# Adding the four ranks of expert outputs: quartered loads and one tiled product for a pair of row tiles

## The reference, cut to what matters

```python
out = jnp.zeros_like(xt)
for e in range(E):
    a = _swiglu(xt @ expert_up_w[e].T)
    out = out + cw[:, e:e + 1] * (a @ expert_down_w[e].T)
out = out + _swiglu(xt @ shared_up_w.T) @ shared_down_w.T
...
x = x + gb * ffn          # gb: one row of 256 for each of the two batches
```

## Time and profile before

| what | value |
|---|---|
| median of 3 runs | 631.35 us (630.82 to 632.19) |
| span of the profiled execution | 628.4 us |
| time outside that span, if the execution took the median | 2.95 us |
| TensorE busy | 576.8 us (92%) |
| VectorE busy | 477.5 us (76%) |
| ScalarE busy | 373.5 us (59%) |
| GpSimd busy | 341.5 us (54%) |
| mean granted TensorE clock | 0.986 |

### The profile page before, as it was taken

How to read it: one execution, slowest core, us unless ns; L and a number is a source line. 1 busy time by engine, 2 the same in 40 slices (tenths; PEclk the granted TensorE clock), 3 DMA queues, 4 the chain that set the end, 5 groups by cost and what they waited for, 6 DMA issues and landing times. The chain is left out here.

```text
span 628.4 us, 13726 instructions
## 1 busy us (share of the span) xinstructions
PE 576.8 (92%) x3945; PEld 390.7 (62%) x3945; DVE 477.5 (76%) x1406; ACT 373.5 (59%) x877; POOL 341.5 (54%) x646
## 2 busy tenths in 40 slices
PE   4997899999999999998987798898979999999987
PEld 4885543334343434443342387687869999999964
DVE  4968998888898778686948569799756776667767
ACT  4775576666676656555867564454546666666630
POOL 5114563646567554944648877781345555555550
PEclk9989999999999999997999989999999999999999
DMA  8389669864547480751115143774986444444983
GB/s 288 82 208 247 179 147 221 206 174 109 141 100 219 117 220 26 174 215 55 69 52 187 54 170 121 252 217 140 339 341 198 139 131 130 137 139 137 355 311 125
DMA packets 66083, 107.96 MB, mean 172 GB/s; under 512 B 13513, under 2 KB 52185, under 8 KB 63834
## 3 DMA queue, kind: packets, MB, share of 16 engines
q1 hardware_dynamic: 59146, 87.93, 48.5%
q0 software_dynamic: 6864, 19.15, 7.9%
HBM read 60.90 MB, written 43.88 MB: 167 GB/s over the span
## 5 line engine op out<-in xcount | busy, mean ns | idle before, releaser
L1458 ACT ACTIVATE Pr<-bank 128x512 f32<-128x512 f32 (+3 forms) x384 | 165.7, 494 | 97.9 <-PE bank L2261 94.1
L1574 DVE TENSOR_REDUCE mxA<-bank 128x1 f32<-128x128 f32 (+3 forms) x256 | 112.3, 482 | 20.9 <-PE bank L2148 20.6
L2261 PE MATMUL bank<-Qs,Ks 99*128 99x512 bf16 (+3 forms) x384 | 118.0, 331 | 6.0 <-ACT Pr L1458 4.2
L2148 PE MATMUL bank<-Ks,Qs 96*128 96x512 bf16 (+3 forms) x384 | 120.2, 330 | 1.2 <-DVE mxB L1574 0.6
L1280 POOL DMA_INDIRECT expert_rows<-Y,YIX x79 | 77.3, 978 | 78.5 <-ACT Y L1521 75.4
L1574 DVE TENSOR_REDUCE mxB<-bank 128x1 f32<-128x512 f32 x128 | 81.6, 681 | 13.8 <-PE bank L2148 13.8
L2247 PE MATMUL bank<-Pr,Vst 128*32 128x512 f32 (+3 forms) x768 | 83.0, 505 | 3.5 <-POOL Pr L1259 3.5
L1257 POOL TENSOR_TENSOR tick<-ident 128x1 f32<-128x1 f32 x128 | 25.5, 199 | 106.5 <-ACT Pr L1458 105.6
L2506 PE MATMUL bank<-W,xh 128*128 x316 | 78.0, 328 | 1.1 <-issue 1.1
L1209 POOL DMA_INDIRECT chosen_rows<-Hx,pos x64 | 67.6, 1056 | 19.2 <-issue 19.2
L2261 PEld LDWEIGHTS bank<-Qs,Ks 99*128 99x128 bf16 x384 | 35.9, 98 | 58.4 <-ACT Pr L1458 39.3
(11 more groups left out here) (256 smaller groups left out, 1278.3 us busy)
## 6 DMA issues: line engine op xcount, KB each, us to landing
G<-chosen_rows SPq DMA_DIRECT2D x79, 134.0 KB, 2.2
Z<-expert_rows SPq DMA_DIRECT2D x8, 1024.0 KB, 8.3
W<-expert_words SPq DMA_DIRECT2D x7, 1088.0 KB, 9.5
qk_parts<-AP SPq DMA_DIRECT2D x32, 192.0 KB, 3.1
Wraw<-in_wexp SPq DMA_DIRECT2D x9, 608.0 KB, 5.7
SA<-in_wexp SPq DMA_DIRECT2D x7, 608.0 KB, 4.3
Vst<-Vall SPq DMA_DIRECT2D x8, 512.0 KB, 5.3
expert_words<-SH SPq DMA_DIRECT2D x7, 480.0 KB, 3.6
```

The costliest lines, as they stand in the source:

```text
L1458: nc.scalar.activation(Pr[(2 * s + j // 2) % 4][:, j % 2, 0:w], ebank[p % RING][:, 0:w], ACT.Exp, scale=SCALE).then_inc(exp_done, EXP)
L1574: nc.vector.tensor_reduce(dst, mbank[u % RING][:, 0:w], AX.X, ALU.max).then_inc(m_red, 1)
L2148: nc.tensor.matmul(mbank[u % RING][:, 0:w], Qs[slot][0:NPR, i // TPC, j, (i % TPC) * P:(i % TPC + 1) * P], Ks[slot][0:NPR, j, k0:k0 + w], ...
L2261: nc.tensor.matmul(ebank[p % RING][:, 0:CH - q0], Ks[slot][0:NAUG, j, kt * P:(kt + 1) * P], Qs[slot][0:NAUG, qc, j, q0:CH], start=True, st ...
```

## The change: what it does

- Loads: each rank is loaded by quarters of 32 partitions. Quarter c of rank r (the tokens of 32 output partitions) goes to slot c of `Z`, at the 32 partitions (r + c) mod 4. So slot c holds on its 128 partitions the same 32 x 16 tokens of all four ranks. Ranks 0 to 2 take 4 DMAs of 512 KB each, in place of 2 of 1 MB; the last rank takes 4 parts of 4 row tiles, each of 4 quarters: 16 DMAs of 128 KB. In all 28 DMAs in place of 8, of the same bytes.
- TensorE: `fold` is a 128x32 matrix with ones where partition and column agree modulo 32. For each of the 8 pairs there are four products, one for each slot, of 128x32 by 128x512, each into its own band of 32 partitions of one bank. One product adds the four ranks of a quarter. VectorE makes `fold` once, at block 8 of the loop, from the identity.
- VectorE multiplies each of the 8 banks by the gate (the last in two halves), and adds pairs 0, 1, 3, 5, 7 to `X`; it adds no ranks any more. GpSimd adds pairs 2, 4 and 6 to `X`, behind its last scatter.
- SP issues the outputs in the order of the pairs, behind waits for VectorE's or GpSimd's add.

```diff
-PE_PAIRS, DVE_PAIRS = (1, 2, 4, 6, 7), (0, 3, 5)
-END_ORDER = (0, 3, 1, 2, 5, 4, 6, 7)
-Z_PARTS = 2
+PAIRS = NT // 2
+LAST_PAIR = PAIRS - 1
+POOL_ADDS = (2, 4, 6)
+DVE_ADDS = tuple(k for k in range(PAIRS) if k not in POOL_ADDS)
+QUARTERS, QP = 4, P // 4
+LAST_PARTS = 4
+Z_PARTS = [1] * (SUMS - 1) + [LAST_PARTS]
...
-            n = NT // Z_PARTS
-            queue.dma_start(Z[:, r, i * n:(i + 1) * n, :],
-                            zd[r * T:(r + 1) * T, :].rearrange("(p n) h -> p n h", n=NT)[:, i * n:(i + 1) * n, :]
-                            ).then_inc(z_in[r * Z_PARTS + i], 16)
+            n = NT // Z_PARTS[r]
+            rows = zd[r * T:(r + 1) * T, :].rearrange("(p n) h -> p n h", n=NT)
+            for c in range(QUARTERS):
+                at = (r + c) % QUARTERS * QP
+                queue.dma_start(Z[at:at + QP, c, i * n:(i + 1) * n, :],
+                                rows[c * QP:(c + 1) * QP, i * n:(i + 1) * n, :]
+                                ).then_inc(z_in[sum(Z_PARTS[:r]) + i], 16)
...
-            for k in END_ORDER:
-                if k in DVE_PAIRS:
-                    sp.wait_ge(z_step, ADD_STEPS * (DVE_PAIRS.index(k) + 1))
+            for k in range(PAIRS):
                 tiles = [(2 * k, 2)] if k != LAST_PAIR else [(2 * k, 1), (2 * k + 1, 1)]
                 for t, n in tiles:
-                    if k in PE_PAIRS:
-                        sp.wait_ge(fin_done, PE_PAIRS.index(k) + 1 + t % 2)
+                    if k in POOL_ADDS:
+                        sp.wait_ge(pool_added, POOL_ADDS.index(k) + 1)
+                    else:
+                        sp.wait_ge(fin_done, DVE_ADDS.index(k) + 1 + t % 2)
...
+            def add_gated(k):
+                pool.wait_ge(s_gated, 2 * NC + k + 1)
+                t = slice(2 * k, 2 * k + 2)
+                nc.gpsimd.tensor_tensor(X[:, t, :], X[:, t, :], Z[:, 0, t, :], ALU.add).then_inc(pool_added, 1)
...
+            def make_fold():
+                dve.wait_ge(mp_step, NIT * 9)
+                nc.vector.tensor_reduce(fold, ident[:, :].rearrange("p (c t) -> p t c", c=QUARTERS), AX.X,
+                                        ALU.add).then_inc(fold_made, 1)
...
-            for k in END_ORDER:
-                if k in DVE_PAIRS:
-                    add_pair(DVE_PAIRS.index(k), k)
-                if k in PE_PAIRS and k != LAST_PAIR:
-                    finish(PE_PAIRS.index(k), 0, 2)
+            for k in range(LAST_PAIR):
+                gate_sums(k, 0, 2)
+                if k in DVE_ADDS:
+                    add_gated(k, 0, 2)
             for first in range(2):
-                finish(PE_PAIRS.index(LAST_PAIR), first, 1)
+                gate_sums(LAST_PAIR, first, 1)
+                add_gated(LAST_PAIR, first, 1)
...
-                for r in range(SUMS):
-                    ins = nc.tensor.matmul(allb[i + u][:, 0:n * H], ident[:, :],
-                                           Z[:, r, t:t + n, :].rearrange("p t h -> p (t h)"), start=(r == 0), stop=(r == SUMS - 1))
+                if k == LAST_PAIR:
+                    pe.wait_ge(y_read, NB)
+                for c in range(QUARTERS):
+                    ins = nc.tensor.matmul(allb[k][c * QP:(c + 1) * QP, :], fold,
+                                           Z[:, c, 2 * k:2 * k + 2, :].rearrange("p t h -> p (t h)"), start=True, stop=True,
+                                           skip_group_check=True)
                 ins.then_inc(z_ps, 1)
```

More of the change, by code:

```diff
@@ L331 @@
 COUNT_AT = 8
-PE_PAIRS, DVE_PAIRS = (1, 2, 4, 6, 7), (0, 3, 5)
-LAST_PAIR = NT // 2 - 1
-assert LAST_PAIR in PE_PAIRS and sorted(PE_PAIRS + DVE_PAIRS) == list(range(NT // 2))
-END_ORDER = (0, 3, 1, 2, 5, 4, 6, 7)
-assert END_ORDER[-1] == LAST_PAIR and all(
-    tuple(k for k in END_ORDER if k in pairs) == pairs for pairs in (PE_PAIRS, DVE_PAIRS))
-ADD_STEPS = 4
-Z_PARTS = 2
+PAIRS = NT // 2
+LAST_PAIR = PAIRS - 1
+POOL_ADDS = (2, 4, 6)
+DVE_ADDS = tuple(k for k in range(PAIRS) if k not in POOL_ADDS)
+assert LAST_PAIR in DVE_ADDS
+QUARTERS, QP = 4, P // 4
+assert QUARTERS == SUMS
+LAST_PARTS = 4
+Z_PARTS = [1] * (SUMS - 1) + [LAST_PARTS]
 SP_LOAD, SP_AHEAD = 4, 6
@@ L663, in program @@
         z_ps = sem("z_ps")
-        z_step = sem("z_step")
+        fold_made = sem("fold_made")
+        pool_added = sem("pool_added")
         fin_done = sem("fin_done")
@@ L690, in program @@
         TAB_STEPS = 2 + 2 * len(PLACE_STEPS)
-        assert SUMS * Z_PARTS <= PRE
-        Z_IN = 16 + RAW_IN
+        assert sum(Z_PARTS) <= PRE
+        Z_IN = 16 + RAW_IN * QUARTERS
         def chosen(c):
@@ L699, in load_outputs @@
         def load_outputs(queue, r, i):
-            n = NT // Z_PARTS
-            queue.dma_start(Z[:, r, i * n:(i + 1) * n, :],
-                            zd[r * T:(r + 1) * T, :].rearrange("(p n) h -> p n h", n=NT)[:, i * n:(i + 1) * n, :]
-                            ).then_inc(z_in[r * Z_PARTS + i], 16)
-        def outputs_in(eng, k):
-            for r in range(SUMS):
-                eng.wait_ge(z_in[r * Z_PARTS + 2 * k * Z_PARTS // NT], Z_IN)
+            n = NT // Z_PARTS[r]
[5 more added lines that the diff above has]
+                                ).then_inc(z_in[sum(Z_PARTS[:r]) + i], 16)
+        def outputs_in(eng, k):
+            if k == 0:
+                for r in range(SUMS - 1):
+                    eng.wait_ge(z_in[r], Z_IN)
+            if k % (PAIRS // LAST_PARTS) == 0:
+                eng.wait_ge(z_in[SUMS - 1 + k // (PAIRS // LAST_PARTS)], Z_IN)
         def low_words(eng, ops, k):
@@ L735, in pad_experts, with sums_of @@
                 queue.dma_start(xd[bass.ds(first[e - lo], P), :], padd[e]).then_inc(pad_out, 16)
-        def sums_of(i, first, n):
-            return allb[i + first][:, 0:n * H].rearrange("p (t h) -> p t h", h=H)
+        def sums_of(k, first, n):
+            return allb[k][:, first * H:(first + n) * H].rearrange("p (t h) -> p t h", h=H)
         def gate_of(k):
@@ L1285, in _ @@
                 scatter_block(b)
+            def add_gated(k):
+                pool.wait_ge(s_gated, 2 * NC + k + 1)
+                t = slice(2 * k, 2 * k + 2)
+                nc.gpsimd.tensor_tensor(X[:, t, :], X[:, t, :], Z[:, 0, t, :], ALU.add).then_inc(pool_added, 1)
+            for k in POOL_ADDS:
+                add_gated(k)
         @block.scalar
@@ L2060, in act_low, with gate_sums, add_gated @@
                                         ALU.subtract).then_inc(al_done, 1)
[L2062 to L2076, removed]
-                t = slice(2 * k + first, 2 * k + first + n)
-                dve.wait_ge(z_ps, i + first + 1)
-                nc.vector.tensor_tensor(Z[:, 0, t, :], sums_of(i, first, n), gate_of(k)[:, 0:n, :], ALU.mult).then_inc(s_gated, 1)
-                dve.wait_ge(s_gated, 2 * NC + i + first + 1)
+            def make_fold():
+                dve.wait_ge(mp_step, NIT * 9)
+                nc.vector.tensor_reduce(fold, ident[:, :].rearrange("p (c t) -> p t c", c=QUARTERS), AX.X,
+                                        ALU.add).then_inc(fold_made, 1)
+            def gate_sums(k, first, n):
+                t = slice(2 * k + first, 2 * k + first + n)
+                dve.wait_ge(z_ps, k + 1)
+                nc.vector.tensor_tensor(Z[:, 0, t, :], sums_of(k, first, n), gate_of(k)[:, 0:n, :], ALU.mult).then_inc(s_gated, 1)
+            def add_gated(k, first, n):
+                t = slice(2 * k + first, 2 * k + first + n)
+                dve.wait_ge(s_gated, 2 * NC + k + first + 1)
                 nc.vector.tensor_tensor(X[:, t, :], X[:, t, :], Z[:, 0, t, :], ALU.add).then_inc(fin_done, 1)
@@ L2545, in _, with add_outputs @@
                     down_unit(s - 2)
-            def add_outputs(i, u, n):
-                t = 2 * PE_PAIRS[i] + u
-                for r in range(SUMS):
-                    ins = nc.tensor.matmul(allb[i + u][:, 0:n * H], ident[:, :],
-                                           Z[:, r, t:t + n, :].rearrange("p t h -> p (t h)"), start=(r == 0), stop=(r == SUMS - 1))
+            def add_outputs(k):
+                if k == LAST_PAIR:
[4 more added lines that the diff above has]
+                                           skip_group_check=True)
                 ins.then_inc(z_ps, 1)
-            for i, k in enumerate(PE_PAIRS):
+            pe.wait_ge(fold_made, 1)
+            for k in range(PAIRS):
                 outputs_in(pe, k)
[L2557 to L2561, removed]
+                add_outputs(k)
 def kernel(**inputs):
```

7 lines of the change are left out of this document (5 added, 2 removed).

## The result

The changed kernel takes 644.16 us (median of 4, 642.28 to 645.33) against 631.77 us for the kernel before: a ratio of 1.0202 with a 95% interval of 1.0166 to 1.0239. It is slower by 12.4 us, and 629.0 was forecast. The profiled execution took 643.73 us.

What follows compares the result with a forecast made beforehand. Loads of Z were taken to decide: traffic to 618.0, last rank's first part at 611.6, first gate 612.7, plus VectorE's 11.1 and output 2.28 gives span 626.1, 2.3 saved: 629.0 us from 631.35, range 624.0 to 636.0.

Steps and rivals of the forecast that it cites:

- Products: TensorE's sums after the loop: eight pairs of four 32-column products take 7.0 us in place of 17.44.
- VectorE's chain: Gates and adds at the end: 9.1 us plus 2.0 us of waits for GpSimd's adds, 11.1 us.
- The outputs at no cost: Outputs stand behind all loads in SP's queue, and were claimed to add no time.
- The loads' rate: Loads of Z into 32 partitions: 242 GB/s, 230 beside scatters, so 36.5 us and traffic ending at 618.0.
- rival D: Slower case: queue bound, scatters take their full 16%, loads average 204 GB/s; 638, or 635.5 with half that share; chance 0.15.
- No gap in the loads: SP's queue: ranks 2 and 3 are issued while earlier ranks still move, so Z's traffic never pauses.
- My sign for the forecast: Profile check at the loop's end: TensorE should wait for Z after 607.8.
- The loop's end at 607.7: TensorE's loop was taken to end when it did before, at 607.7, with the loads deciding what follows.
- The last sentence of my prediction: Forecast is wrong if late scatters stall the loop through four Y tiles, TensorE's last block ending after 609; no case given.
- the 218 GB/s of the Trainium skill: Page's figure for partitions 0 to 31, weighed against the change: traffic would end at 620.0, estimate 631.0.

Runs made afterwards that it cites:

- e10: Changed kernel, rank r loaded to every fourth partition (4j + r), 4 KB rows, 16 DMAs, all adds on VectorE: 626.43 us, 0.9916 of the kernel before.
- e12: e10 with the adds of pairs 2, 4 and 6 given back to GpSimd: 631.81 us, 1.0008 of the kernel before.
- e5: Changed kernel with every load in quarters of 32 neighbouring partitions in 4 KB rows, and no adds on GpSimd: 635.54 us, 1.0045 of the kernel before.
- e6: Kernel before, plus a one-column GpSimd memset of a spare tile behind VectorE's last add but one: 638.17 us, ratio 1.0071.
- e7: Changed kernel with whole loads over 128 partitions (16 KB rows, sums not the reference's) and no GpSimd adds: 626.67 us, 0.9897 of the kernel before.
- e2: Changed kernel with all eight pairs added by VectorE, none by GpSimd: 637.03 us, 1.0072 of the kernel before.
- e11: Changed kernel with only the ranks' place altered to every fourth partition, 16 KB rows, GpSimd's adds kept: 633.73 us, 1.0029 of the kernel before.
- e1: Kernel before with each load of Z cut into four DMAs of 32 partitions, nothing else altered: 641.32 us, ratio 1.0156.
- e4: Changed kernel with ranks 0 to 2 loaded in two parts each (8 KB rows), still in quarters: 637.59 us, 1.0089 of the kernel before.
- e3: Changed kernel with whole loads over 128 partitions (16 KB rows, sums not the reference's), GpSimd's adds kept: 632.74 us, 1.0008 of the kernel before.

## Why the prediction was wrong, step by step

The forecast was 629.0 with a range of 624 to 636; the kernel took 644.16, above the range and on the other side of no change.

- **Products: right.** 7.0 us for the eight groups was forecast from the attention's products; at full clock they take 7.38 us together (e10). In after the first half ran at a lower clock, which no step of mine had, since I let TensorE run without a pause.
- **VectorE's chain: right.** 9.1 us and 2.0 us of waits for GpSimd, 11.1 in all. After's first gate starts at 622.5, its last add ends at 633.67: 11.2 us, with a wait of 0.29 us for TensorE's slowed products in it; e12 needs 10.77 us. The waits are where they were forecast: VectorE's adds beside GpSimd's take 1.08, 1.27 and 1.26 us. Here are two of them:

```profile
628.08 1.27 DVE L2090 TENSOR_TENSOR Z<-bank,GBr 128x512 f32<-128x512 f32 x2
629.38 1.27 DVE L2096 TENSOR_TENSOR X<-X,Z 128x512 f32<-128x512 f32 x1
...
631.62 1.26 DVE L2096 TENSOR_TENSOR X<-X,Z 128x256 f32<-128x256 f32 x1
```

- **The outputs at no cost: right.** SP is done 2.1 us behind VectorE's last add, as before.
- **The loads' rate: the term was too good by a fifth.** I took 242 GB/s for loads into 32 partitions and gave the scatters nearly nothing of it, so 230 for `Z`. Alone the loads moved 220 (582 to 589 of after). With scatters all traffic stayed at 250 to 266 (e5), of which `Z` got 191. I had argued that a scatter writes DRAM and leaves the load's target free; it took 19.5% of the engines' time all the same. That was rival D's ground, and D comes nearest of the rivals where nothing else stops the loop and GpSimd adds nothing: the kernel then takes 635.54 us (e5), and D had 635.5 with half the scatters' share (its sum done again gives 635.9) and 638 with all of it. That it comes so near is partly luck: D had 204 GB/s for all traffic, where e5 has 250 to 266; e5's products take 9.31 us at a lowered clock (0.56 in 618 to 624), which D lacked, and e5 has no waits for GpSimd's adds, which D had. I gave it 0.15, against the averages of 193 to 204 that I called the firmer rows myself.
- **No gap in the loads: wrong, for a reason outside the sum.** Rank 2 was to be issued at 593.3 and rank 3 at 602.2. SP waits before each rank until that rank's scattered rows have landed; with the loop late, rank 2 was issued at 601.07, and the late scatter held rank 3 until 614.05. The stretch 614 to 616 moves 123 GB/s. So in after the loads' rate no longer shows in the end by itself: TensorE's products followed the loop directly and had no wait for `Z`. My sign for the forecast, that TensorE would wait for `Z` after 607.8, failed in after and held in e5.
- **The loop's end at 607.7: wrong, the largest term.** All of my sum stood on a loop that ends when it did before. It ends at 620.61, 11.9 us of it behind the start of the loads (1.0 us of the 12.9 was there before them). Against the same blocks of before the two stalls make 9.3 us of these 11.9; the rest is in the blocks behind them, of which the last three are about 0.5 us longer each, at the granted clock of 0.50. The last sentence of my prediction names the mechanism, a scatter behind a slow queue and the ring of four `Y` tiles, and says that it had no case. It should have had the largest one of the slower side. The row for it was at hand: the same stretch of before shows the scatters' queue silent for 4 us when the first load begins, which is half of the ring's 8 us.
- **The DRAIN: not thought of.** I asked only when GpSimd's adds end, not what GpSimd does after its last instruction. The DRAIN of 10.4 us stood in the trace of before, hidden. It costs 5.9 us of after's span, 5.4 us of e12's median and, by itself, 5.6 us of e6's span.

By the runs the change's parts are worth this: the products, gates and `fold` -4 to -5 us (e7 and e10 against before); the adds on GpSimd with their DRAIN +5.4 (e12 against e10) to +7.1 (after against e2); the place of the ranks in quarters +10.4 (after against e11, whose stall by 16 KB rows is still in it).

**What is shown and what is not.** It is shown that 32 neighbouring partitions in each DMA slow the loads (e1 against before, after against e11), that in quarters longer rows keep the scatters silent for longer (after, e4, e5), and that the DRAIN follows GpSimd's last instruction (e6). How an engine takes turns between the two queues isn't shown. Read in steps of 0.25 us, q0 has no packet for 7.25 us in after (rows of 16 KB), 3.5 and 2.75 us in e4 and e1 (8 KB) and 1.75 us in e5 (4 KB). Where the loads have the full rate, the silence doesn't follow the row: 4.5 and 4.25 us with 16 KB (e3, e11), 4.5 with 8 KB (before), 4.0 with 4 KB (e10). What grows with the row there is the time that the next scatter then needs for its 48 packets: 2.25 and 2.5 us in e3 and e11, 1.75 in before, 1.0 in e10. In the seven microseconds of after the loads have about 94 packets over 2 KB, some 6 rows of 16 KB for each of 16 engines, before a scatter's packet moves; in 584 to 587 of e3 65, some 4 of 16 KB; in the four of before about 159, some 10 of 8 KB; in 584 to 587 of e10 about 176, some 11 of 4 KB. The Trainium skill (DMA: Bandwidth & Descriptors, Queues, rings and completion order) says that an engine goes round its queues and takes a packet of typically 9 to 17 descriptors from one before it turns to the next. If a row is a descriptor, the counts of 10 and 11 fit that and those of 4 and 6 lie below it; no run here counts the turns themselves, so this cause of the silence stays open.

The Trainium skill (SBUF — State Buffer, Door 1: The DMA port swizzle) gives 8 of 16 ports to partitions 0 to 31, and by its formula all 16 to every fourth partition. The 220 GB/s of quarters and the 316 to 375 GB/s of e10 agree with both. The Trainium skill (SBUF — State Buffer, "Can I just issue two DMAs to hit both halves?") says, as my prediction weighed, that two transfers at once on different partitions gained only 6%. The quarters of after, which go to different partitions one after the other and move at 220 GB/s, agree with it. By the 218 GB/s of the Trainium skill my estimate would have been 631.0, which is still 13 us short, because the time went into the late scatters and the DRAIN.

## What to carry to other kernels

Before a load is reshaped, ask which other transfers stand behind it on the same DMA engines and how many microseconds of delay their buffers allow: here a ring of four tiles allowed 8 us, and long rows at half the rate took 12. If an operation needs operands on fewer partitions, spread them over the whole range (every fourth) rather than take a block of neighbours; it cost nothing here and gave the rate back. Don't give the last work of a kernel to GpSimd unless more than its DRAIN (here 9 to 12 us) follows on other engines.

## What the runs showed of the hardware that I had not expected

- GpSimd's DRAIN at the program's exit takes 9.3 us (e6) to 12.0 us (e1), 10.4 in most runs, even behind a memset of one column of 0.10 us (e6); ScalarE's and VectorE's take about 0.5 us and SP's 7 ns.
- The scatters on GpSimd's software queue move nothing while a newly issued load on SP's queue moves its first rows: for 7.25 us with quarters in rows of 16 KB (after), 3.5 us with 8 KB (e4), 1.75 us with 4 KB (e5), and 4.0 to 4.5 us at the full rate with rows of 4 to 16 KB (e10, before, e3, e11). The ordinary gap between two scatters, about 1 us, is part of each of these.
- 32 partitions can be loaded at 316 to 375 GB/s, scatters included, when they are every fourth (e10, rows of 4 KB; 408 and 424 in e11, rows of 16 KB), against 250 to 266 when they are neighbours (e5), even where successive loads go to different neighbours.
- An add on GpSimd beside VectorE's lengthens VectorE's add of two SBUF tiles from 0.69 to 1.27 us; three adds moved from VectorE to GpSimd saved VectorE 0.2 us in all.
